# Gate logits taken by token tiles, the route in two parts, row statistics and lows moved between engines

## What is computed

```
x = x + xattn(layernorm(x), ctx)   # cross attention, folded projections
x = x + ssm(layernorm(x))          # inner layernorm, gate z, long convolution by FFT
                                   # y = clip(y @ out_w.T + out_b + residual, -10, 10)
x = x + ffn(layernorm(x))          # mixture of 8 experts, the best one per token:
    logits = xt @ gate_w + gate_b
    sel = argmax(softmax(logits))
    out = xt @ expert_w[sel] + expert_b[sel]
```

## Time and profile before

| | us |
|---|---|
| median of 3 runs | 1134.09 (1133.72 to 1135.25) |
| the profiled execution | 1134.54 |
| its span | 1132.8 |
| PE, DVE, ACT, POOL busy | 1093.9, 841.3, 530.5, 537.5 |

### The profile page before, as it was taken

One profiled execution on the slowest core, in us unless ns is written; L12 is line 12 of the kernel. 1 busy time (PEld: TensorE's weight loads), 2 busy tenths in 40 slices (PEclk: granted clock), 3 DMA queues, 4 the chain that ended last, 5 costly groups with the idle time before them and its releaser, 6 DMA issues.

```text
span 1132.8 us, 16497 instructions
## 1 busy us (share of the span) xinstructions
PE 1093.9 (97%) x4969; PEld 884.5 (78%) x4969; DVE 841.3 (74%) x1756; ACT 530.5 (47%) x1127; POOL 537.5 (47%) x588
## 2 busy tenths in 40 slices
PE   7999999999999999999999999999999999998498
PEld 5787877878888888888888888888888888886375
DVE  6963498799888888778357777776777657699584
ACT  4221056556555555533464444444444444356462
POOL 3700445345444544411266666665765632177253
PEclk8999999999999999999999999999999999999699
DMA  8211368977876787432429767766876541025991
GB/s 292 84 53 59 52 153 211 218 194 190 204 179 185 190 192 195 140 87 99 76 73 203 193 187 202 187 191 171 213 185 177 179 161 38 1 76 161 323 398 66
DMA packets 199351, 182.26 MB, mean 161 GB/s; under 512 B 17873, under 2 KB 144881, under 8 KB 199299
## 3 DMA queue, kind: packets, MB, share of 16 engines
q1 hardware_dynamic: 178658, 140.21, 48.3%
q10 hardware_dynamic: 17280, 31.46, 7.9%
q0 software_dynamic: 3360, 9.97, 2.4%
HBM read 141.73 MB, written 41.68 MB: 162 GB/s over the span
## 4 chain that ended last, share of the span: by engine, by line
PE 80%; DVE 8%; POOL 4%; DMA 3%; issue 3%; SPq 1%; ACT 1%; POOLq 0%; ACTq 0%; DVEq 0%
PE bank L644 39%; PE bank L783 28%; PE bank L1040 4%; PE bank L837 3%; PE bank L652 1%; PE bank L1026 1%; DMA stage<-in_L_xattn_hW_dram 1%; DVE h L1527 1%; DMA stage<-in_L_ffn_expert_w_dram 1%; DMA spectra<-in_ctx_dram 1%; PE bank L987 1%; PE bank L678 1%; POOL hl_C L2023 1%; PE bank L1045 1%; POOL hl_B L2039 1%
## 5 line engine op out<-in xcount | busy, mean ns | idle before, releaser
L1187 ACT ACTIVATE probs<-bank,nbias 128x512 f32<-128x512 f32 x128 | 88.1, 688 | 242.3 <-DVE nbias L1650 242.1
L783 PE MATMUL bank<-hl_F,probsT 128*128 128x512 f32 x768 | 190.4, 397 | 0.6 <-issue 0.4
L783 PE MATMUL bank<-hl_A,probsT 128*128 128x512 f32 x768 | 190.4, 396 | 0.0
L644 PE MATMUL bank<-hl_B,hl_D 128*128 128x512 f32 x768 | 185.7, 391 | 1.8 <-POOL hl_B L2039 1.4
L1645 DVE TENSOR_REDUCE mx<-bank 128x1 f32<-128x512 f32 x128 | 88.0, 687 | 133.9 <-PE bank L644 133.9
L644 PE MATMUL bank<-hl_C,hl_D 128*128 128x512 f32 x768 | 185.3, 390 | 0.0
L783 PEld LDWEIGHTS bank<-hl_F,probsT 128*128 128x128 f32 x768 | 144.1, 188 | 35.4 <-issue 0.8
L783 PEld LDWEIGHTS bank<-hl_A,probsT 128*128 128x128 f32 x768 | 144.1, 188 | 34.3 <-POOL hl_A L2032 0.2
L644 PEld LDWEIGHTS bank<-hl_B,hl_D 128*128 128x128 f32 x768 | 143.7, 188 | 34.1 <-issue 2.3
L644 PEld LDWEIGHTS bank<-hl_C,hl_D 128*128 128x128 f32 x768 | 144.1, 188 | 31.7 <-issue 0.3
L2032 POOL TENSOR_TENSOR hl_F<-stage,hl_F 128x512 fp32r<-128x512 f32 x64 | 84.7, 1323 | 162.2 <-ACT hl_F L1152 162.1
(11 more groups left out here) (419 smaller groups left out, 1862.6 us busy)
## 6 DMA issues: line engine op xcount, KB each, us to landing
p_rows<-probs ACTq DMA_DIRECT2D x120, 256.0 KB, 3.1
stage<-in_ctx_dram SPq DMA_DIRECT2D x112, 256.0 KB, 3.2
spectra<-in_ctx_dram SPq DMA_DIRECT2D x64, 256.0 KB, 5.9
xb<-in_ctx_dram SPq DMA_DIRECT2D x64, 256.0 KB, 5.9
resid<-p_rows SPq DMA_DIRECT2D x240, 64.0 KB, 2.1
h<-p_rows SPq DMA_DIRECT2D x120, 64.0 KB, 2.5
obB<-p_rows SPq DMA_DIRECT2D x120, 64.0 KB, 2.0
stage<-in_L_ffn_expert_w_dram SPq DMA_DIRECT2D x6, 1024.0 KB, 6.9
```

What stands on the lines that cost most here:

```text
L644: last = nc.tensor.matmul(dst, lhs[:, a, t, k * P:(k + 1) * P], rhs[:, c, t, :], start=(t == 0 and (a, c) == PASSES[0]), stop=(t == T - 1 ...
L783: last = nc.tensor.matmul(obank[u % 2][:], probsT[u % 2][:, a, j, :], nat[b][par][:, c, j, :], start=(j == 0 and (a, c) == PASSES[0]), sto ...
L1187: nc.scalar.activation(dst, src, ACT.Exp, bias=nbias[:, q:q + 1], scale=SCALE, accum_out=rsum[:, q:q + 1]).then_inc(probs_ready, 1)
```

## The change

- PE takes the logits tile by tile with the turned tokens as the stationary side and gate_w (8 columns) as the moving side, straight into the bank `logit_columns`; the two `logits` jobs, ScalarE's copies of them and `turn_logits` are gone. PE's order is turn 0, 1, 2, logits 0, turn 3, logits 1, and so on.
- ScalarE takes the sums and squares of tiles 0 to 2 of batch 1 as well: one sum before `weights(3)`, the rest behind it, between the copies of the turned tiles. VectorE keeps the last tile.
- `route()` gives the rows of the 8 first tiles (`slots.0`, from the rank alone) and then those of the spare tiles (`slots.1`). GpSimd's first eight gathers wait for the first part, its scatters for the second. `split_expert_bias` moves behind `route()`.
- The first batch's gated lows go from GpSimd to VectorE, between product groups 2 and 3. GpSimd's masks become two short instructions made from `lanes`, and its W0 lows go ahead of `add_out_bias(1)`, behind the wait for the last product.
- PE turns group 1 after the first three matmuls of mix(0), no longer before them.

```diff
-             + tiles_at(0, "x_ssm")[2:] + tiles_at(1, "x_ssm") + tiles_at(0, "ffnT") + tiles_at(1, "ffnT")[:2]
-             + ["logits@0"] + tiles_at(1, "ffnT")[2:] + ["logits@1", "logit_columns", "ranks", "slots"] + MIX_JOBS)
+             + tiles_at(0, "x_ssm")[2:] + tiles_at(1, "x_ssm") + tiles_at(0, "ffnT") + tiles_at(1, "ffnT")
+             + ["logit_columns", "ranks"] + (["slots.0", "slots.1"]) + MIX_JOBS)
...
+                for n in range(B * T + 2):
+                    if n < B * T:
+                        turn_ffn(n // T, n % T)
+                    if n >= 2:
+                        gate_logits(n - 2)
                 rank_tokens()
-                place_tokens()
+                place_tokens("slots.0", 1, 0, E)
+                place_tokens("slots.1", 2, E, E)
                 turn_tokens(0)
                 for g in range(GROUPS):
-                    if g + 1 < GROUPS:
+                    if 0 < g < GROUPS - 1:
                         turn_tokens(g + 1)
                     mix(g)
...
+            def gate_logits(n):
+
+                dst = bank_of("logit_columns")
+                if n == 0:
+                    open_bank("logit_columns")
+                evacuated_from(f"ffnT.{n % T}@{n // T}")
+                for k in range(T):
+                    last = nc.tensor.matmul(dst[:, n * E:(n + 1) * E], spectra[:, n, k * P:(k + 1) * P], gate_raw[:, k, :],
+                                            start=(k == 0), stop=(k == T - 1))
+                if n == B * T - 1:
+                    last.then_inc(filled, 1)
...
+            def place_tokens(job, count, first, width):
+
+                pe.wait_ge(ranked, count)
+                dst = open_bank(job)
                 for n in range(B * T):
-                    last = nc.tensor.matmul(dst[:, 0:2 * E], place[:, n, :], numbered[:, n, :], start=(n == 0), stop=(n == B * T - 1))
+                    last = nc.tensor.matmul(dst[:, 0:width], place[:, n, :], numbered[:, n, first:first + width],
+                                            start=(n == 0), stop=(n == B * T - 1))
                 last.then_inc(filled, 1)
...
+                    if g == 0 and t == 0:
+                        turn_tokens(1)
...
+            def summing(ins):
+
+                summed[0] += 1
+                ins.then_inc(row_summed, 1)
+                act.wait_ge(row_summed, summed[0])
+
+            def sum_rows(n):
+
+                evacuated_by(act, f"x_ssm.{n % T}@{n // T}")
+                summing(nc.scalar.activation(h[0][:], xb[:, n // T, n % T, :], ACT.Copy, accum_out=row_sum[:, n:n + 1]))
+
+            def square_rows(ns):
+
+                of = slice(ns[0], ns[-1] + 1)
+                summing(nc.scalar.activation(centre[:, of], row_sum[:, of], ACT.Copy, scale=-1.0 / D))
+                for n in ns:
+                    summing(nc.scalar.activation(h[0][:], xb[:, n // T, n % T, :], ACT.Square, bias=centre[:, n:n + 1],
+                                                 accum_out=spread[:, n:n + 1]))
+
+            def means(ns):
+
+                of = slice(ns[0], ns[-1] + 1)
+                nc.scalar.activation(mv_out[:, of, 0], row_sum[:, of], ACT.Copy, scale=1.0 / D)
+                nc.scalar.activation(mv_out[:, of, 1], spread[:, of], ACT.Copy, scale=1.0 / D).then_inc(means_ready, 1)
...
-                means()
+                square_rows(range(T))
+                means(range(T))
+                sum_rows(T)
                 weights(3)
-                turned_ffn(0, range(T))
-                turned_ffn(1, range(2))
-                copy_logits(0)
-                turned_ffn(1, range(2, T))
-                copy_logits(1)
+                sum_rows(T + 1)
+                square_rows(range(T, T + 2))
+                turned_ffn(0, range(2))
+                sum_rows(T + 2)
+                square_rows(range(T + 2, T + 3))
+                means(range(T, 2 * T - 1))
+                turned_ffn(0, range(2, T))
+                turned_ffn(1, range(T))
...
+            def last_row_statistics():
+
+                dve.wait_ge(evacuated, EVAC["x_ssm.3@1"])
+                link(row_statistics(xb[:, 1], T - 1))
+                link(nc.vector.bn_aggr(mv_out[:, 2 * T - 1, :], bnst[:, T - 1, :]))
...
+                link(nc.vector.tensor_reduce(rank, hit_value, AX_X, ALU.add))
+                place_at(rank)
                 link(nc.vector.tensor_tensor(above, count.unsqueeze(2).to_broadcast([P, E, SPARE]),
                                              limits.unsqueeze(1).to_broadcast([P, E, SPARE]), ALU.is_gt))
                 link(nc.vector.tensor_reduce(tiles_over, above, AX_X, ALU.add))
-                nc.vector.tensor_tensor(above, rank.unsqueeze(2).to_broadcast([P, B * T, SPARE]),
-                                        limits.unsqueeze(1).to_broadcast([P, B * T, SPARE]), ALU.is_ge)
                 link(nc.vector.tensor_tensor_scan(tiles_upto, unit, tiles_over, 0.0, ALU.mult, ALU.add))
+                filled_by(dve, "slots.0")
+                nc.vector.tensor_scalar(gather_rows[:, 0:E], bank_of("slots.0")[:, 0:E], float(FAR), float(TOKENS - 1),
+                                        ALU.add, ALU.min).then_inc(indexed, 1)
+                nc.vector.tensor_scalar(scatter_rows[:, 0:E], bank_of("slots.0")[:, 0:E], float(FAR), None, ALU.add).then_inc(evacuated, 1)
...
+                place_at(lane)
+                choose_experts()
+                filled_by(dve, "slots.1")
+                nc.vector.tensor_scalar(gather_rows[:, E:GROUPS], bank_of("slots.1")[:, 0:SPARE], float(FAR), float(TOKENS - 1),
+                                        ALU.add, ALU.min).then_inc(indexed, 1)
+                nc.vector.tensor_scalar(scatter_rows[:, E:GROUPS], bank_of("slots.1")[:, 0:SPARE], float(FAR), None, ALU.add).then_inc(evacuated, 1)
...
-                outputs(1, range(1, 5))
+                outputs(1, range(1, 3))
+                for k in range(T):
+                    gated_lo(0, k)
+                outputs(1, range(3, 5))
...
+                last_row_statistics()
+                dve.wait_ge(means_ready, 2)
                 scale_outputs()
-                split_expert_bias()
                 gate()
                 route()
+                split_expert_bias()
...
+                pool.wait_ge(iota_made, 1)
+                nc.gpsimd.tensor_scalar(ones, lanes, 0.0, 1.0, ALU.mult, ALU.add).then_inc(table_made, 1)
+                nc.gpsimd.tensor_scalar(before, lanes, partition, None, ALU.is_gt).then_inc(table_made, 1)
...
                 routing_numbers()
                 add_out_bias(0)
-                gated_lo()
                 routing_masks()
+                pool.wait_ge(product_step, PRODUCTS * (TRIPS + 2))
+                lo_tiles("W0", raw[BUF["W0"]], weights_hl[0])
                 add_out_bias(1)
-                for g in range(EARLY):
+                for g in range(1, EARLY):
                     lo_tiles(f"W{g}", raw[BUF[f"W{g}"]], weights_hl[g])
...
                 pool.wait_ge(indexed, 1)
                 for g in range(ROWS_KEPT):
                     gather(g)
+                pool.wait_ge(indexed, 2)
                 for g in range(GROUPS):
```

More of the change, by code:

```diff
@@ L96, in kind @@
     return name.split(".")[0].split("@")[0]
-COPIED_KINDS = ("z", "Kar", "Kai", "GT", "U0r", "U0i", "U1r", "U1i", "gate_sums", "ffnT", "logits")
+COPIED_KINDS = ("z", "Kar", "Kai", "GT", "U0r", "U0i", "U1r", "U1i", "gate_sums", "ffnT")
 COPIED = {name: k + 1 for k, name in enumerate(n for n in JOBS if kind(n) in COPIED_KINDS)}
@@ L979, in turn_ffn @@
                 last.then_inc(filled, 1)
-            def gate_logits(b, parts):
-                dst = open_bank(f"logits@{b}")
-                n = T // parts
-                for m in range(parts):
-                    evacuated_from(f"ffnT.{n * m + n - 1}@{b}")
-                    for k in range(T):
-                        last = nc.tensor.matmul(dst[0:E, n * m * P:n * (m + 1) * P], gate_raw[:, k, :],
-                                                spectra[:, T * b + n * m:T * b + n * (m + 1), k * P:(k + 1) * P],
-                                                start=(k == 0), stop=(k == T - 1))
-                last.then_inc(filled, 1)
-            def turn_logits():
-                dst = open_bank("logit_columns")
-                for b in range(B):
-                    evacuated_from(f"logits@{b}")
-                    for k in range(T):
-                        col = (b * T + k) * E
-                        last = nc.tensor.transpose(dst[:, col:col + E], logitT[b][:, k * P:(k + 1) * P], ident[0:E, 0:E])
-                last.then_inc(filled, 1)
+            def gate_logits(n):
[8 more added lines that the diff above has]
+                    last.then_inc(filled, 1)
             def rank_tokens():
@@ L2162, in add_out_bias @@
                     nc.gpsimd.tensor_tensor(r, r, outbB[:], ALU.add).then_inc(resid_ready[b], 1)
-            def gated_lo():
-                for k in range(T):
```

(14 more changed lines are left out.)

88 lines of the change are left out of this document (23 added, 65 removed).

## The result

| | median, us | range | runs |
|---|---|---|---|
| before | 1134.67 | 1133.72 to 1135.64 | 4 |
| after | 1142.23 | 1140.14 to 1142.69 | 4 |

The ratio is 1.0055, with a 95% interval of 1.004 to 1.007: **slower by 7.6 us**, above the predicted range (1130.9 to 1136.9). A second group of runs gave 1.0058 (1.0041 to 1.0075). The profiled execution of after is the fastest of the four, 1140.14 us, with a span of 1138.3. A second profile of the same kernel took 1141.27 us, with a span of 1139.5.

A forecast was written before the change was run, and what follows sets the result against it. PE holds 80% of the chain; ahead of the mixture, W3's landing, logits, routing and gathers set its start. Terms -0.8 + 1.8 + 1.8 - 2.8 - 0.6 + 0.5 = -0.1 gave 1134.0 us (chance 0.40), range 1130.9 to 1136.9.

The forecast's parts named there:

- The gated lows: VectorE's products: four lows at 2.4 us replace a 3.2 us excess spent waiting on GpSimd; net -0.8 us.
- the port rival: GpSimd's four W0 lows alternate with VectorE's four L1810, pushing each by 1.07: +3.9 us, 1137.9; chance 0.12.
- The first copy: ScalarE's first ffnT copy, after rounding W3 and the added statistics: done 5.5 us after W3's start, at 1040.6.
- The route: First index needs only the rank, so `place` runs at 1054.35 where it ran at 1057.19: -2.8 us.
- From index to mixture: First index to mix(0), with VectorE's second route part and bias split between: 9.1 against 8.6, +0.5 us.
- The clock: PE idles 5.2 us before the logits, clock falls to 1.2 GHz, returns after 4.6 us of work: +1.8 us.
- Rank matmuls at full clock: Nine rank matmuls in the route run at full clock if it rose late in the logits: -0.6 us.
- W3 earlier by 0.8: Through earlier lows, store and issue, W3 starts on ScalarE at 1035.15 instead of 1035.95.
- clock rivals: Clock stays up in the logits, 1132.2, chance 0.15; or is up through first slot product too, 1131.2, chance 0.20.
- three signs: Wrong if clock reads 1.00 across logits, VectorE's lows at 1009 are stretched, or mix(0) waits for a gather, not VectorE.
- Gathers late: W6 and W7 loads overlap the gathers, low at G (first index) + 10.1: +1.7 us, 1135.7; chance 0.13.
- It doesn't do what it says: First indices come early but norm stores or DMA hold the gathers; counted in the late-gathers rival, no chance of its own.

The follow-up runs named there:

- the wide filler: Changed kernel plus discarded 128x512 matmuls on PE: 22 before the first logits (1.0014), or those and 2 after each of the first 7 tiles' logits (1.0008).
- the narrow filler: Changed kernel plus 40 discarded 128x8 matmuls on PE in the wait before the first logits; 1.0063 to the kernel before, 1143.14 us.
- route and gated lows: Kernel before plus route in two parts, moved bias split and group 1 turn, gated lows on VectorE, GpSimd's new order; logits and statistics as before: 0.9998, 1135.76 us.
- logits alone: Kernel before plus only the logits by tokens, with their order of turns and copies; 1.003, 1139.47 us.
- logits without the statistics: Changed kernel with all of batch 1's row statistics left on VectorE; 1.0024 to the kernel before, 1138.56 us.
- filler in the wait: Changed kernel plus 22 discarded 128x512 matmuls on PE between the third turn and the first logits; 1.0014 to the kernel before, 1136.20 us.
- tokens with the clock held: Changed kernel, statistics left on VectorE, plus discarded 128x512 matmuls: 12 before the logits, one after each of seven tiles, 47 through the route; 0.9986, 1133.98 us.

## Why the prediction was wrong, step by step

**Right.** The gated lows: predicted -0.8; L1810 starts at 1005.56, with the 3.26 at 1008.82 against 1009.53, -0.7. No product of VectorE waited, the lows at L1810 took 1.28 a pair beside GpSimd's W0 lows, and the port rival did not come:

```profile
1005.56 1.28 DVE L1810 TENSOR_TENSOR hl_D<-spectra,hl_D 128x512 fp32r<-128x512 f32 x2
...
1005.71 7.23 POOL L2032 TENSOR_TENSOR hl_C<-stage,hl_C 128x512 fp32r<-128x512 f32 x4 [21.43 <-DVE spectra L375]
```

The first copy was predicted 5.5 us after W3's start, and the first logit stands at 5.51; the third copy at 8.6, and it ended at 8.4 (1041.0). A tile of logits at full clock was priced 0.9 and a turn 0.46; where the wide filler kept the clock they took 0.79 and 0.49. The route: `place` 2.84 earlier after the logits was predicted; it is 4.96 us after them (1060.72) instead of 7.60, so 2.64. From index to mixture +0.5, measured +0.67, by the mechanism that was named: the low of the first turned tile stands right behind the bias split (1071.75, 1072.42).

**Wrong: the step "The clock".** It had the fall right and the return wrong: it priced the lost clock at 1.8 us, and 7.8 was lost. I let the clock come back 4.6 us after PE took up work, the middle of 3.5 and 5.8. The first is the mixture's return, from 128x512 matmuls; the second comes from a stretch at 11.9 whose work I had not looked at, and it is of the same kind: 24 matmuls of 128x512 from 11.86 on (TensorE's timeline of before). None of the work ahead of either return was like that of the logits. The clock did not return in 17.6 us. Two levels make a simple price: each us at 0.50 costs half of itself while PE is the bound. By the sum, the last logit should have come 15.3 + 1.8 = 17.1 us after W3's start, and came after 23.14: 6.0 too little. In the chain of after the first tile takes 1.85, four more 1.51, five turns 0.95 and the last three tiles 4.93: 17.6 us, and 5.51 + 17.6 = 23.1. That is the whole of it. The four kinds of row, in order of time:

```profile
1038.13 1.85 PE bank L984 x8
1039.97 0.95 PE bank L974 x4
1040.92 1.51 PE bank L984 x8
...
1050.73 4.93 PE bank L984 x24
```

The Trainium skill, "TensorE: Matmul & The Clock Gate", "What's actually happening", says that the gate is set by how busy TensorE has been. The row 1038.10:1055.70 has TensorE busy 17.53 of 17.60 us at 0.50: taken with the busy time of a profile, that rule would have had the clock back, and the measurement is against it. The same page, "Part 4: PE-mode transpose", says that transposes don't count as busy in that way. The 24 matmuls at the end of the logits and the narrow filler were no transposes and did no better; whether the turns between helped or not, no run here separates.

**The same term, twice more.** "Rank matmuls at full clock", -0.6, hung on the return: they took 1.45 for seven, and the stretch from logits to index gave 2.56 and not 3.4. And the mixture was priced as before; the clock came back 6.1 us into it instead of 3.5, half of 2.6 is 1.3, and +1.25 is what the table has. In the second profile it came back after 4.0, half of 0.5 is 0.25, and the mixture took 0.33 longer: this term is partly luck of the execution.

**W3 earlier by 0.8**: it came 0.07 earlier. Its issue did come earlier, at 1024.43 or 1027.69 with the 3.26, against 1028.13: 0.44. The landing then took 8.2 us instead of 7.8. In other profiles the transfer took 7.8 to 9.2 us in the chain (before, route and gated lows, logits alone, logits without the statistics), so a gain of under 1 us ahead of it can't be counted on.

Put together: 6.0 (clock in the logits) + 0.84 (route) + 1.25 (mixture) + 0.73 (W3) + 0.17 (index to mixture) = 9.0, against 8.8 - (-0.1) = 8.9 between the measured stretch and the sum.

**The rivals.** Two were clock rivals, and both let it be *better* than the forecast. The one that happened was missing: that it does not come back at all. "Gathers late" and "It doesn't do what it says" were right for route and gated lows without the rest: the gather landed after 7.21 us, close to the 7.1 of the rival, and the store held it by 0.4. In the changed kernel the logits were so late that the index was the last thing again, and the first gather landed in about 5 us. The route's 2.6 us there repair a part of what the logits lose. None of the three signs that the prediction named for being wrong appeared: the clock row says 0.50 across the logits, the lows at L1810 were not stretched, and mix(0) waited for VectorE. A sign for "the clock doesn't come back" was not among them.

## What to carry to other kernels

Price a stretch of small matmuls at the clock that such matmuls have had in a trace, not at the clock of the wide ones near it: where no wide filler stood ahead of the logits or among them, the 128x8 matmuls ran here at half clock for as long as they lasted, 17.5 to 17.7 us in five traces, however full PE's busy row was. Before work is put on an engine between a load and the consumer of its copies, count how many copies the consumer needs first: the same statistics came to 4.7 us where the logits needed four copies, and to 2.7 where they needed one. An index that comes earlier is worth only what the store and the DMA behind it let through. And where TensorE waits a few us at a time ahead of a long run of wide matmuls, it is worth a try to fill the waits with wide matmuls that are thrown away: here that alone gave 0.9976, more than any part of the change.

## What the runs showed of the hardware

- With TensorE busy 4.80 of 4.80 us with 128x8 matmuls and turns, the granted clock fell from 1.00 to 0.50 (filler in the wait).
- Under 128x512 matmuls a lost clock rose after 3.3 us (route and gated lows, 1037.7 to 1041.0), 3.5 us (the mixture of before), 4.0 and 6.1 us (the two profiles of after, in the mixture), and 9.1 us (1049.1 to 1058.2, tokens with the clock held, with rank matmuls between the wide ones). Nothing that the profile shows tells these apart.
- A wait of 2.8 us did not bring the clock down in before. It fell 2.5 us into a wait of 5.7 us in the first profile of after, 3.0 into 4.0 with the logits alone, and 2.9 into 3.0 with route and gated lows. Waits of nearly one length had both outcomes.
- The first gather took 4.6 us to land in before, and 6.1 to 8.2 us in four runs in which it started 0.9 to 2.6 us earlier after W3's start; PE had the first gathered tile 30.3 to 31.9 us after W3's start in all five.
- The two profiles of after differ by 2.35 us in when they reach the same instruction (982.51 and 984.86), so a profile's own total says little about 3 us; its stretches from a common instruction say more.
